# Attention inside a fused kernel: low-rank columns joined to the values, maxima turned in one transpose, masks and products in another order

## The chip, the cores and the metric

One core of one Trainium2 chip. The metric is the device time of one execution in microseconds.

## The reference, cut to what matters

Eight sequences of 512 rows by 512 columns pass through a state-space block `s` and, beside it, a transformer block whose gated output multiplies it. The change lies in the transformer block's attention and in the small low-rank modulation of its gate:

```python
x = _rmsnorm(hidden_states, ln1_w)
attn = _attention(x, Wq, Wk, Wv, Wo)      # 16 heads of 32, causal, softmax
mod = MOD_SCALE * jnp.tanh(attn @ A)      # A is 512 x 16
h = _rmsnorm(residual, ln2_w)
gate_pre = h @ W_in_base.T + mod * (h @ A) @ B
gate = jax.nn.silu(gate_pre)
up = h @ W_up_base.T
mlp_out = gate * up @ W_down.T
return residual + mlp_out
```

`attn` is needed only as `attn @ A`, so the kernel folds Wv, Wo and A into 16 columns a head: the values have 16 heads x 16 = 256 columns.

## The kernel before, in words

The kernel has three stages: the state-space block (to about 821 us), attention (to about 1462 us) and the feed-forward part with the output. FP32 products are made as three FP32R matmuls each: high by high, high by low, low by high (`project3`, lines 72 to 74). "Batch" below is one of the 8 sequences.

In attention each engine walks one list, `steps` (lines 1369 to 1453). It is laid out by hand: `at(third, kind, ...)` puts a step into a third of a head; a head has three thirds, a batch of 16 heads has 48, a word w is four heads. Within a third the order is that of the `at` calls. Each engine takes from the list the steps that concern it, strictly in order; semaphores join them. Per head:

- **weights**: key blocks J against queries, transposed scores into banks 4 and 5. The thirds hold J = 0 (512 columns), J = 1 and 3 (384 + 128), J = 2 (256). Behind each product one bf16 matmul of the identity with a triangle of 0 and -1e30 adds the causal mask to the 128 diagonal columns (lines 1747 to 1753). ScalarE takes the exponential (L1851), then casts all 1280 columns to FP16 (L1856). VectorE subtracts to get the remainder (L1922); POOL does its last 256 columns in the first seven batches (L2016).
- **largest**: six heads ahead, the untransposed scores (L1730) into banks 2 and 3, query block 3 (512 columns), then 2 and 0 (384 + 128), then 1 (256). VectorE masks them and takes the row maximum, one instruction a block (L1915), into `MX`. TensorE may write a bank again when the third two before has been reduced (`maxima`, L1725).
- **largest_in**, **largest_out**, once a word: four transposes turn `MX` (L1738), ScalarE negates them into a 4x512 tile (L1835), and a DMA puts them as row 96 under the queries (L1843), so that the weights' product subtracts the maximum.
- **mixed**: two heads later, the FP16 probabilities (high and remainder) times the bf16 values, 20 matmuls of 50 columns (L1768, L1770). It comes last in the first third of a head. **drawn**, **inverse**, **divided**, **summed**, **gathered** divide by the row sums and add up the heads.

Between them, for the next batch, in banks 0 and 1: **normal** (transposes of the input, thirds -3 to 3), **project** (queries and keys, L1707 to L1709), **values** (thirds 14, 17, 26, 35; 256 columns, through `project3`), and **low_rank** (third 45): 12 matmuls that give `h @ A` turned, as 16x512, which ScalarE copies to `HA` (L1830). Banks 0 and 1 pass from user to user by the list `frees01`. VectorE turns copies into remainders (L1891, L1898, L1905).

**modulation**, once a batch, third 11 of the batch that follows (third 17 for batch 6, in the feed-forward list for batch 7): four transposes of the summed attention `AM` (L1796), tanh to a 16x512 tile (L1879), VectorE multiplies it by 0.1 and `HA` (L1957), ScalarE copies it twice to `MS` (L1884, L1885), VectorE stores the remainder (L1962).

The feed-forward stage has its own list (`ffn_order`, L2056); its TensorE is busy nearly all the time. The last batch's modulation stands there after column 4.

Of the kernel before, what the change touches and what calls it, by code (L numbers as in the profile page):

```python
# [32 lines left out]
def build(nc, x, WinT, convw, convb, WxT, Alog, dtb, outWT, Dp, ln1, ln2, WqT, WkT, Wv, Wo, Aw, Bw, WgT, WuT, WdT,  # L33
          ident, umask, arow, maskt, maskT, out):
    ctx = ExitStack()
    with ctx:
# [1229 lines left out]
        def fast_pool(pool):  # L1266
# [38 lines left out]
        (a_xs, a_tr, a_rh, a_rl, a_pj, a_qh, a_ql, a_vl, a_vh, a_v1, a_vp, a_lr, a_ha, a_lg, a_mx, a_ti, a_ni, a_wt, a_ex, a_ph,  # L1305
         a_rm, a_rp, a_pv, a_ao, a_nu, a_sm, a_tm, a_th, a_mo) = sems(
            "a_xs a_tr a_rh a_rl a_pj a_qh a_ql a_vl a_vh a_v1 a_vp a_lr a_ha a_lg a_mx a_ti a_ni a_wt a_ex a_ph "
# [18 lines left out]
        VW = [sb(at_, f"VW{i}", [128, 4, 256], F32R) for i in range(2)]  # L1326
        AW = [sb(at_, f"AW{i}", [128, 4, R], F32R) for i in range(2)]
# [17 lines left out]
        NM = [sb(at_, f"NM{i}", [4, S], F32R) for i in range(2)]  # L1345
        HA = [sb(at_, f"HA{i}", [R, S]) for i in range(2)]
# [3 lines left out]
        TH = sb(at_, "TH", [R, S])  # L1350
# [18 lines left out]
        for third in range(-72, 3 * HEADS + 24):  # L1369
            g, p = divmod(third, 3)  # L1370
            if 0 <= g < HEADS:
                at(third, "weights", third, ((0,), (1, 3), (2,))[p])
            if 0 <= g + 6 < HEADS:
                at(third, "largest", third + 18, ((3,), (2, 0), (1,))[p])
# [5 lines left out]
            if p == 0 and 0 <= g - 2 < HEADS:  # L1380
                at(third, "mixed", g - 2)
            if p == 1 and g % 2 and 0 <= g - 3 < HEADS:
                at(third, "drawn", (g - 3) // 2)
        for b in range(NB):
# [22 lines left out]
            bank_of["low_rank", b] = 1  # L1407
            at(t + (45 if b else 44), "low_rank", b)
# [47 lines left out]
        for kind, a, how in steps:  # L1456
# [6 lines left out]
            elif kind == "low_rank":  # L1463
                key, free = (kind, a), (a_ha, a + 1)
            elif kind == "largest_in":
                key, free = (kind, a), (a_ni, a + 1)
            elif kind == "modulation":
                key, free = (kind, a), (a_th, 3 * a + 1)
# [10 lines left out]
        maxima = [1, 3, 4]  # L1479
# [70 lines left out]
        def prep_scalar(act, part):  # L1550
# [7 lines left out]
            if part == 5:  # L1558
                for k in range(4):
                    act.wait_ge(a_pp, 2 + k // 2)  # L1560
                    act.activation(VW[0][:, k, :], values_weights(k), ACT.Identity, scale=L1C[:, k:k + 1]).then_inc(a_pa, 1)
            if part == 6:
                for k in range(4):
                    act.activation(AW[0][:, k, :], AF[:, k, :], ACT.Identity, scale=L2C[:, k:k + 1]).then_inc(a_pa, 1)
# [873 lines left out]
```

## Time and profile before

| | us |
|---|---|
| median of 3 runs | 2537.52 |
| lowest, highest | 2536.71, 2538.83 |
| span of the profiled execution | 2534.2 |
| median less that span | 3.3 |
| TensorE busy in the span | 2475.4 |
| VectorE busy | 1370.8 |
| ScalarE busy | 1060.8 |
| POOL busy | 474.7 |

The profiled execution is known by its span, from the first to the last instruction of the program; its own whole time is not listed, so it is set beside the median of the runs. Busy time is the union of an engine's instructions. TensorE's ends are modelled, and its matmuls overlap: the pace is the distance between two starts. PE, PEld, DVE, ACT and POOL are TensorE, its weight loads, VectorE, ScalarE and GpSimd; L1730 is a line of the kernel.

### The profile page before, as it was taken

How to read it: one execution, taken by the hardware profiler on the slowest of the kernel's cores; microseconds unless marked ns; L12 is line 12 of the kernel's file. 1: busy time of each engine (PE TensorE's matmuls, PEld its weight loads, DVE VectorE, ACT ScalarE, POOL GpSimd, SP SyncE). 2: the span in 40 equal slices, each digit the busy share in tenths (PEclk: the TensorE clock that was granted, in tenths of full speed). 3: DMA queues.
4: the chain of work that ended last, by engine and by line, in shares of the span. 5: the costliest groups of instructions: out<-in, count | busy, mean ns of one | idle time of the engine just before them, and what ended most of it. 6: DMA issues, size and time to landing. Idle time of an engine off the chain costs nothing.

```text
span 2534.2 us, 38406 instructions
## 1 busy us (share of the span) xinstructions
PE 2475.4 (98%) x14359; PEld 1996.5 (79%) x14359; DVE 1370.8 (54%) x2860; ACT 1060.8 (42%) x1767; POOL 474.7 (19%) x430
## 2 busy tenths in 40 slices
PE   7999999999999999999999899999999999999998
PEld 5878888878878777777777678888888788888887
DVE  7756757667655688888888842122224323222323
ACT  6444454544544477777777731111112211111111
POOL 4000000000002254444443600000000202222222
PEclk9999999999999999999999999999999999999999
DMA  4010100000003776666666320111113312222212
GB/s 143 18 34 1 34 34 1 34 17 18 17 17 114 222 205 183 199 195 177 192 179 166 106 88 28 44 51 50 50 50 125 125 46 96 100 96 100 96 67 83
DMA packets 106971, 228.12 MB, mean 90 GB/s; under 512 B 14976, under 2 KB 15488, under 8 KB 100624
## 3 DMA queue, kind: packets, MB, share of 16 engines
q1 hardware_dynamic: 105056, 225.31, 27.9%
q8 instruction: 120, 1.97, 0.3%
q14 instruction: 67, 0.55, 0.1%
q10 hardware_dynamic: 1728, 0.29, 0.1%
HBM read 149.77 MB, written 75.50 MB: 89 GB/s over the span
## 4 chain that ended last, share of the span: by engine, by line
PE 89%; DVE 6%; issue 3%; ACT 2%; DMA 0%; POOL 0%; SPq 0%; DVEq 0%; ACTq 0%; POOLq 0%
PE PS L72 14%; PE PS L74 14%; PE PS L73 13%; PE PS L2227 4%; PE PS L2228 4%; PE PS L2229 4%; PE PS L1730 3%; PE PS L1749 3%; PE PS L1707 3%; PE PS L811 2%; PE PS L812 2%; PE PS L813 2%; PE PS L1709 2%; PE PS L1708 2%; PE PS L797 1%
## 5 line engine op out<-in xcount | busy, mean ns | idle before, releaser
L2296 DVE TENSOR_TENSOR SG<-SG,PS 128x512 f32<-128x512 f32 x124 | 85.2, 687 | 642.1 <-PE PS L74 640.1
L74 PE MATMUL PS<-FH,GU 128*128 128x512 f32 x992 | 388.7, 392 | 0.0
L72 PE MATMUL PS<-FH,GU 128*128 128x512 f32 x992 | 387.8, 391 | 0.2 <-DVE DW L2287 0.2
L73 PE MATMUL PS<-FL,GU 128*128 128x512 f32 x992 | 387.9, 391 | 0.0
L1915 DVE CUSTOM_DVE_ANT_0 PS<-PS,MK 128x512 f32<-128x512 f32 (+3 forms) x512 | 243.6, 505 | 86.0 <-PE PS L1730 85.0
L2266 ACT ACTIVATE SG<-PS 128x512 f32<-128x512 f32 x124 | 74.0, 597 | 466.8 <-PE PS L2203 465.2
L2332 POOL TENSOR_SCALAR XN<-XT,MEAN,RSTD 128x512 f32<-128x512 f32 x32 | 69.5, 2171 | 940.0 <-DMA M<-m_scratch 940.0
L1851 ACT ACTIVATE PF<-PS 128x512 f32<-128x512 f32 (+1 forms) x384 | 199.4, 526 | 79.9 <-PE PS L1751 78.4
L2269 ACT CAST GH<-SG 128x512 fp32r<-128x512 f32 x124 | 76.9, 620 | 349.6 <-DVE SG L2296 349.6
L72 PEld LDWEIGHTS PS<-FH,GU 128*128 128x128 f32 x992 | 186.7, 188 | 41.1 <-ACT SG L2266 0.6
L73 PEld LDWEIGHTS PS<-FL,GU 128*128 128x128 f32 x992 | 186.6, 188 | 40.9
L74 PEld LDWEIGHTS PS<-FH,GU 128*128 128x128 f32 x992 | 186.8, 188 | 39.9
L72 PE MATMUL PS<-XH,WH 128*128 128x512 f32 x504 | 208.9, 415 | 0.0
L2227 PE MATMUL PS<-DW,GH 128*128 128x512 f32 x500 | 195.5, 391 | 4.1 <-DVE GL L2298 4.1
L74 PE MATMUL PS<-XH,WL 128*128 128x512 f32 x504 | 197.7, 392 | 0.0
L73 PE MATMUL PS<-XL,WH 128*128 128x512 f32 x504 | 197.0, 391 | 0.0
L2229 PE MATMUL PS<-DW,GL 128*128 128x512 f32 x500 | 195.4, 391 | 0.0
L2228 PE MATMUL PS<-DW,GH 128*128 128x512 f32 x500 | 195.4, 391 | 0.0
L1922 DVE TENSOR_TENSOR PL<-PF,PH 128x1024 f16<-128x1024 f32 (+1 forms) x128 | 178.0, 1391 | 4.7 <-ACT PH L1856 4.7
L1730 PE MATMUL PS<-KS,QS 96*128 96x512 f32 (+3 forms) x512 | 169.9, 373 | 10.8 <-DVE MX L1915 10.6
L1749 PE MATMUL PS<-QS,KS 97*128 97x512 f32 (+3 forms) x512 | 165.4, 353 | 4.4 <-ACT PF L1851 2.7
L1856 ACT CAST PH<-PF 128x1280 f16<-128x1280 f32 x128 | 161.3, 1260 | 4.1
(299 smaller groups left out, 5312.6 us busy)
## 6 DMA issues: line engine op xcount, KB each, us to landing
qk_scratch<-QT SPq DMA_DIRECT2D x128, 256.0 KB, 4.6
QS<-qk_scratch SPq DMA_DIRECT2D x96, 256.0 KB, 4.0
KS<-qk_scratch SPq DMA_DIRECT2D x96, 256.0 KB, 4.1
FH<-rh_scratch SPq DMA_DIRECT2D x16, 1024.0 KB, 5.8
FL<-rl_scratch SPq DMA_DIRECT2D x16, 1024.0 KB, 7.7
XF<-in_x_dram SPq DMA_DIRECT2D x32, 256.0 KB, 4.1
s_scratch<-ZS SPq DMA_DIRECT2D x8, 1024.0 KB, 4.3
rh_scratch<-RH SPq DMA_DIRECT2D x8, 1024.0 KB, 10.2
```

Source lines behind the costliest of these rows:

```text
L72: pe.matmul(o, lh(k), xh(k), start=open_ and k == 0, stop=False, skip_group_check=True)
L73: pe.matmul(o, lh(k), xl(k), start=False, stop=False, skip_group_check=True)
L74: last = pe.matmul(o, ll(k), xh(k), start=False, stop=close and k == nk - 1, skip_group_check=True)
L1730: t = pe.matmul(p[:, at:at + n], QS[0:96, h, 128 * k:n], KS[0:96, h, 0:n], start=True, stop=True, skip_group_check=True)
L1749: pe.matmul(p[:, at:at + n], KS[0:97, h, 128 * J:128 * J + 128], QS[0:97, h, 128 * J:512], start=True, stop=False, skip_group_check=True)
L1851: act.activation(PE_[u][:, o:o + at], PS[4 + a % 2][:, 0:at], ACT.Exp, scale=SC).then_inc(a_ex, 1)
L1856: act.copy(PH[u][:, :], PE_[u][:, :]).then_inc(a_ph, 1)
L1915: dve.tensor_tensor_reduce(out=p[:, at:at + n], in0=p[:, at:at + n], in1=MK[:, 512 - n:512], scale=1.0, scalar=NEG, op0=ALU.add, op1=ALU.m ...
L1922: dve.tensor_tensor(PL[u][:, 0:n], PE_[u][:, 0:n], PH[u][:, 0:n], ALU.subtract).then_inc(a_rm, 1)
L2227: pe.matmul(PS[4 + k][:, :], GH[g][:, c], DW[:, f, 0, :], start=f == 0, stop=False, skip_group_check=True)
L2228: pe.matmul(PS[4 + k][:, :], GH[g][:, c], DW[:, f, 1, :], start=False, stop=False, skip_group_check=True)
L2229: t = pe.matmul(PS[4 + k][:, :], GL[g][:, c], DW[:, f, 0, :], start=False, stop=f == 7, skip_group_check=True)
```

## The change

1. Low rank: `A` becomes 16 more columns of the values' weights `VW` (272 columns), and the step `low_rank` goes. ScalarE copies the 16 columns of each of the four row blocks to `HA`, now 128 x 4 x 16. VectorE's `values_low` waits for it too.
2. Modulation in the same layout: tanh on 128x64 (`bounded`, third 10), times `HA` (`modulated`, third 11), then the four transposes (third 20, bank 0; batch 6 as before third 17 in bank 1), copies and remainder straight from the bank.
3. Maxima: `MX` is ordered so that one transpose turns all 16 columns; the negated tile is 16x128.
4. `mixed` is first in its third, ahead of weights.
5. Query block 0 of the maxima moves from the second third to the last, ahead of that third's weights; it opens the bank, and block 1 joins it behind the weights. `maxima` is 1, 2, 4 in place of 1, 3, 4.
6. Masks: with one key block the mask matmul comes first and opens the bank; with two (J = 1 and 3) one matmul of two 128-column blocks, 256 columns apart, closes it. Three mask matmuls a head in place of four.

```diff
@@ in the layout of the steps @@
         for third in range(-72, 3 * HEADS + 24):
             g, p = divmod(third, 3)
+            if p == 0 and 0 <= g - 2 < HEADS:
+                at(third, "mixed", g - 2)
+            if p == 2 and 0 <= g + 6 < HEADS:
+                at(third, "largest", third + 18, 0)
             if 0 <= g < HEADS:
                 at(third, "weights", third, ((0,), (1, 3), (2,))[p])
             if 0 <= g + 6 < HEADS:
-                at(third, "largest", third + 18, ((3,), (2, 0), (1,))[p])
+                at(third, "largest", third + 18, (3, 2, 1)[p])
...
-            if p == 0 and 0 <= g - 2 < HEADS:
-                at(third, "mixed", g - 2)
...
-            bank_of["low_rank", b] = 1
-            at(t + (45 if b else 44), "low_rank", b)
...
-            m, bank_of["modulation", b] = (107, 0) if b + 2 < NB else (113, 1)
+            m, bank_of["modulation", b] = (116, 0) if b + 2 < NB else (113, 1)
             if b + 1 < NB:
+                at(t + 106, "bounded", b)
+                at(t + 107, "modulated", b)
                 at(t + m, "modulation", b)
-                at(t + m + 1, "modulated", b)
-                at(t + m + 2, "modulation_out", b)
-                at(t + m + 3, "modulation_low", b)
+                at(t + m + 1, "modulation_out", b)
+                at(t + m + 2, "modulation_low", b)
...
-        maxima = [1, 3, 4]
+        maxima = [1, 2, 4]
@@ TensorE @@
-                    project3(pe, p[:, 0:256], lambda k: RH[:, k, c], lambda k: RL[:, k, c],
+                    project3(pe, p[:, 0:272], lambda k: RH[:, k, c], lambda k: RL[:, k, c],
                              lambda k: VW[0][:, k, :], lambda k: VW[1][:, k, :], 4).then_inc(a_vl, 1)
-                elif kind == "low_rank":
-                    p = own01(kind, a)
-                    project3(pe, p[0:R, :], lambda k: AW[0][:, k, :], lambda k: AW[1][:, k, :], rh, rl, 4).then_inc(a_lr, 1)
                 elif kind == "largest":
                     w, j = divmod(a // 3, 4)
-                    h, at, p = 4 * (w % 4) + j, 0, PS[2 + a % 2]
-                    if a >= 2:
+                    h, at, n = 4 * (w % 4) + j, 256 if how == 0 else 0, 128 * how + 128
+                    if a >= 2 and how != 1:
                         pe.wait_ge(a_mx, 4 * ((a - 2) // 3) + maxima[(a - 2) % 3])
...
-                    for k in how:
-                        n = 128 * k + 128
-                        t = pe.matmul(p[:, at:at + n], QS[0:96, h, 128 * k:n], KS[0:96, h, 0:n], start=True, stop=True,
-                                      skip_group_check=True)
-                        at += n
-                    t.then_inc(a_lg, 1)
+                    t = pe.matmul(PS[2 + a % 2][:, at:at + n], QS[0:96, h, 128 * how:n], KS[0:96, h, 0:n], start=how != 1, stop=True,
+                                  skip_group_check=True)
+                    if how:
+                        t.then_inc(a_lg, 1)
                 elif kind == "largest_in":
                     p = own01(kind, a)
                     pe.wait_ge(a_mx, 16 * a + 16)
-                    for k in range(4):
-                        t = pe.transpose(p[0:4, 128 * k:128 * k + 128], MX[a % 2][:, k, :], idn[:, :])
-                    t.then_inc(a_ti, 1)
+                    pe.transpose(p[0:16, 0:128], MX[a % 2][:, :, :].rearrange("p j k -> p (j k)"), idn[:, :]).then_inc(a_ti, 1)
...
+                    blocks = p[:, :].rearrange("p (c q) -> p c q", q=128)[:, 0:len(how) * 3 - 2:3, :]
+                    triangles = MR[:, :].unsqueeze(1).to_broadcast([128, len(how), 128])
+                    if len(how) == 1:
+                        pe.matmul(blocks, idb[:, :], triangles, start=True, stop=False, skip_group_check=True)
                     for J in how:
                         n = 512 - 128 * J
-                        pe.matmul(p[:, at:at + n], KS[0:97, h, 128 * J:128 * J + 128], QS[0:97, h, 128 * J:512],
-                                  start=True, stop=False, skip_group_check=True)
-                        t = pe.matmul(p[:, at:at + 128], idb[:, :], MR[:, :], start=False, stop=True, skip_group_check=True)
+                        t = pe.matmul(p[:, at:at + n], KS[0:97, h, 128 * J:128 * J + 128], QS[0:97, h, 128 * J:512],
+                                      start=len(how) == 2 and at == 0, stop=len(how) == 1, skip_group_check=True)
                         at += n
+                    if len(how) == 2:
+                        t = pe.matmul(blocks, idb[:, :], triangles, start=False, stop=True, skip_group_check=True)
                     t.then_inc(a_wt, 1)
...
                 elif kind == "modulation":
                     p = own01(kind, a)
-                    pe.wait_ge(a_sm, sm(4 * a + 3, 4))
+                    pe.wait_ge(a_mo, 2 * a + 1)
                     for k in range(4):
-                        t = pe.transpose(p[0:R, 128 * k:128 * k + 128], AM[:, k, :], idn[:, :])
+                        t = pe.transpose(p[0:R, 128 * k:128 * k + 128], TH[:, k, :], idn[:, :])
@@ ScalarE @@
                 elif kind == "values":
...
+                    if a >= 2:
+                        act.wait_ge(a_mo, 2 * (a - 2) + 1)
+                    act.copy(HA[a % 2][:, how, :], bank01(kind, a, how)[:, 256:272]).then_inc(a_ha, 1)
...
+                elif kind == "bounded":
+                    act.wait_ge(a_sm, sm(4 * a + 3, 4))
+                    act.wait_ge(a_tm, a)
+                    act.activation(TH[:, :, :], AM[:, :, :], ACT.Tanh).then_inc(a_th, 1)
@@ VectorE @@
                 elif kind == "largest":
...
-                    for k in how:
-                        n = 128 * k + 128
-                        dve.tensor_tensor_reduce(out=p[:, at:at + n], in0=p[:, at:at + n], in1=MK[:, 512 - n:512], scale=1.0,
-                                                 scalar=NEG, op0=ALU.add, op1=ALU.max,
-                                                 accum_out=MX[w % 2][:, k, j:j + 1]).then_inc(a_mx, 1)
-                        at += n
+                    dve.tensor_tensor_reduce(out=p, in0=p, in1=MK[:, 512 - n:512], scale=1.0, scalar=NEG, op0=ALU.add,
+                                             op1=ALU.max, accum_out=MX[w % 2][:, j, how:how + 1]).then_inc(a_mx, 1)
...
                 elif kind == "modulated":
                     dve.wait_ge(a_th, 3 * a + 1)
-                    dve.wait_ge(a_ha, a + 1)
-                    dve.scalar_tensor_tensor(out=TH[:, :], in0=TH[:, :], scalar=0.1, in1=HA[a % 2][:, :],
+                    dve.wait_ge(a_ha, 4 * a + 4)
+                    dve.scalar_tensor_tensor(out=TH[:, :, :], in0=TH[:, :, :], scalar=0.1, in1=HA[a % 2][:, :, :],
                                              op0=ALU.mult, op1=ALU.mult).then_inc(a_mo, 1)
```

## Rows read from the trace of the kernel before

**Rows 1.** The page, part 1: busy time, share of the span, instructions.

```profile
PE 2475.4 (98%) x14359; PEld 1996.5 (79%) x14359; DVE 1370.8 (54%) x2860; ACT 1060.8 (42%) x1767; POOL 474.7 (19%) x430
```

**Rows 2.** Windows: stretch, length, busy time of each engine, granted clock, DMA share, GB/s.

```profile
857.00:860.40 3.40, 3.40 (x13) 2.46 (x14) 2.44 (x10) 1.17 (x2) 0.00 (x0) 0.52 1.00 408
...
1070.48:1106.03 35.55, 34.65 (x338) 25.80 (x336) 30.95 (x88) 27.43 (x47) 14.46 (x16) 1.00 0.68 194
1030.87:1070.48 39.61, 38.91 (x371) 30.89 (x369) 33.05 (x89) 29.86 (x50) 19.92 (x22) 1.00 0.62 184
1388.24:1462.12 73.88, 65.24 (x645) 49.54 (x645) 63.14 (x131) 53.59 (x88) 48.22 (x42) 0.98 0.35 109
```

**Rows 3.** Waits of TensorE from 864 to 1388 us: total, times, longest.

```profile
PE PS L1730 <- DVE MX L1915: 5.4, 9, 0.7
```

**Rows 4.** Timeline of TensorE: start, duration, instruction.

```profile
1000.21 0.48 PE L1707 MATMUL PS<-RH,QW 128*128 128x512 f32 x1
1000.53 0.39 PE L1708 MATMUL PS<-RL,QW 128*128 128x512 f32 x1
...
1000.99 0.34 PE L1749 MATMUL PS<-QS,KS 97*128 97x384 f32 x1
1001.17 0.23 PE L1751 MATMUL PS<-MR,idb 128*128 128x128 bf16 x1
1001.21 0.31 PE L1749 MATMUL PS<-QS,KS 97*128 97x128 f32 x1
1001.36 0.23 PE L1751 MATMUL PS<-MR,idb 128*128 128x128 bf16 x1
1001.40 0.48 PE L1730 MATMUL PS<-KS,QS 96*128 96x384 f32 x2
1001.72 0.44 PE L1707 MATMUL PS<-RH,QW 128*128 128x512 f32 x1
1002.00 0.40 PE L1708 MATMUL PS<-RL,QW 128*128 128x512 f32 x1
...
1003.54 0.39 PE L1749 MATMUL PS<-QS,KS 97*128 97x512 f32 x1
1003.77 0.23 PE L1751 MATMUL PS<-MR,idb 128*128 128x128 bf16 x1
1003.81 0.48 PE L1730 MATMUL PS<-KS,QS 96*128 96x512 f32 x1
...
1004.13 0.20 PE L1768 MATMUL PS<-VB,PH 128*128 128x50 bf16 x1
```

**Rows 5.** Timeline of TensorE: the transposes of the maxima, four in one row.

```profile
1004.65 0.60 PE L1738 MATMUL PS<-idn,MX 128*4 128x128 f32 x4
```

**Rows 6.** Timelines around the low rank: TensorE's first, its successor, VectorE's instruction behind it.

```profile
1008.67 0.39 PE L72 MATMUL PS<-RH,AW 128*16 128x512 f32 x1
...
1011.42 0.60 PE L1697 MATMUL PS<-idn,STGB 128*128 128x128 f32 x4
...
1012.79 0.57 DVE L1915 CUSTOM_DVE_ANT_0 PS<-PS,MK 128x384 f32<-128x384 f32 x1 [2.01 <-PE PS L1730]
```

**Rows 7.** Timeline of TensorE: products of the values, before the first head.

```profile
829.11 0.28 PE L72 MATMUL PS<-VW,RH 128*128 128x256 f32 x1
829.22 0.28 PE L73 MATMUL PS<-VW,RH 128*128 128x256 f32 x1
```

**Rows 8.** Groups from 988 to 1064 us: ScalarE's copy of the values.

```profile
L1821 ACT CAST VB<-PS 128x256 bf16<-128x256 f32 x4 | 1.5, 370 | 1.2 <-PE PS L74 1.2
```

**Rows 9.** Timeline at the last modulation, in the feed-forward stage.

```profile
1474.54 0.68 DVE L2287 TENSOR_TENSOR DW<-STGC,DW 128x512 fp32r<-128x512 f32 x1
...
1476.10 0.60 PE L1796 MATMUL PS<-idn,AM 128*16 128x128 f32 x4
```

**Rows 10.** Timelines of POOL and TensorE: a remainder and the products behind it.

```profile
1090.37 1.71 POOL L2016 TENSOR_TENSOR PL<-PF,PH 128x256 f16<-128x256 f32 x1 [6.08 <-ACT PH L1856]
...
1092.73 0.20 PE L1768 MATMUL PS<-VB,PH 128*128 128x50 bf16 x1
```

More of the change, by code:

```diff
@@ L1325, in build @@
         QW = [sb(at_, f"QW{i}", [128, 4, 512], F32R) for i in range(4)]
-        VW = [sb(at_, f"VW{i}", [128, 4, 256], F32R) for i in range(2)]
-        AW = [sb(at_, f"AW{i}", [128, 4, R], F32R) for i in range(2)]
+        VW = [sb(at_, f"VW{i}", [128, 4, 256 + R], F32R) for i in range(2)]
         STGB = sb(at_, "STGB", [128, 2048])
@@ L1344, in build @@
         MX = [sb(at_, f"MX{i}", [128, 4, 4]) for i in range(2)]
-        NM = [sb(at_, f"NM{i}", [4, S], F32R) for i in range(2)]
-        HA = [sb(at_, f"HA{i}", [R, S]) for i in range(2)]
+        NM = [sb(at_, f"NM{i}", [16, 128], F32R) for i in range(2)]
+        HA = [sb(at_, f"HA{i}", [128, 4, R]) for i in range(2)]
         on = ExitStack()
@@ L1349, in build @@
         on.close()
-        TH = sb(at_, "TH", [R, S])
+        TH = sb(at_, "TH", [128, 4, R])
         RD = sb(at_, "RD", [128, 16])
@@ L1467, in build @@
             elif kind == "modulation":
-                key, free = (kind, a), (a_th, 3 * a + 1)
+                key, free = (kind, a), (a_mo, 2 * a + 2)
             elif kind == "gate" and how == 0:
@@ L1598, in prep_vector @@
                     dve.wait_ge(a_pa, 10 + k // 2 * 2)
-                    low(VW[1][:, k, :], values_weights(k), L1C[:, k:k + 1], VW[0][:, k, :])
+                    low(VW[1][:, k, 0:256], values_weights(k), L1C[:, k:k + 1], VW[0][:, k, 0:256])
             if part in (5, 6):
@@ L1610, in prep_vector @@
                     dve.wait_ge(a_pa, k + 13)
-                    low(AW[1][:, k, :], AF[:, k, :], L2C[:, k:k + 1], AW[0][:, k, :])
+                    low(VW[1][:, k, 256:272], AF[:, k, :], L2C[:, k:k + 1], VW[0][:, k, 256:272])
             if part == 8:
@@ L1825, in attn_scalar @@
                     act.copy(BS[32 * a:32 * a + 16, :], STGA[1][0:R, :]).then_inc(a_pa, 1)
-                elif kind == "low_rank":
-                    act.wait_ge(a_lr, a + 1)
-                    if a >= 2:
-                        act.wait_ge(a_mo, 2 * (a - 2) + 1)
-                    act.copy(HA[a % 2][:, :], bank01(kind, a)[0:R, :]).then_inc(a_ha, 1)
                 elif kind == "largest_in":
@@ L1908, in attn_vector @@
                     w, j = divmod(a // 3, 4)
-                    at, p = 0, PS[2 + a % 2]
+                    n, at = 128 * how + 128, 256 if how == 0 else 0
+                    p = PS[2 + a % 2][:, at:at + n]
                     dve.wait_ge(a_lg, a + 1)
@@ L1933, in attn_vector @@
                     dve.wait_ge(a_sm, sm(a, 2))
-                    dve.wait_ge(a_tm, a // 4)
+                    if a % 4 == 0 and a:
+                        dve.wait_ge(a_th, 3 * (a // 4) - 2)
                     dve.tensor_reduce(dst[:, :, :], NU[:, :, :].rearrange("p (h k) r -> p k r h", k=4), AX.X,
```

38 lines of the change are left out of this document (16 added, 22 removed).

## The prediction

> **What bounds the kernel now.** I first read the shares of the page: TensorE is busy 98% of the span, VectorE 54%, ScalarE 42% [rows 1]. That average mixes stages. The change touches only the attention stage (about 821 to 1462 us), so I cut it with the window view: into one batch of 16 heads, 75.2 us, in two stretches, and the last batch. In the first stretch, 35.55 us, the last four heads of one batch and the first four of the next, TensorE is busy 34.65 and VectorE 30.95. In the second, 39.61 us, the eight heads between, they are busy 38.91 and 33.05 [rows 2]. So TensorE sets the time in both, but in the first VectorE is only 4.6 us behind. Then the waits: over seven batches TensorE waits for VectorE's maxima 5.4 us [rows 3]. Last the timeline of TensorE, because "busy" there hides weight loads: a matmul is listed from its issue, so what counts is the distance from one start to the next.
>
> **Order and masks, per head, on TensorE.** In the first third of a head a 512-column product takes 0.23 (1003.54 to 1003.77), the 128-column mask 0.04, and the 512-column product behind it 0.32 (1003.81 to 1004.13): 0.09 of it is the FP32 weight load that so short a matmul cannot cover. The products with the values are as short, and the projection after them takes 0.32 too (1000.21 to 1000.53) [rows 4]. Afterwards the values come first, the mask follows them and the key product pays one uncovered load for both: 0.09 saved. In the second third 0.99 to 2.00 is 1.01 us: 384 columns 0.18, mask 0.04, 128 columns 0.15, mask 0.04, then 384 and 128 columns 0.32, and the projection's first 0.28 [rows 4]. Afterwards: 0.18, 0.06 for 128 columns, the joined mask of 256 columns, 384 columns 0.18, projection 0.23. No row shows a two-block bf16 matmul; it is at least its neighbour's 0.04 and at most two masks with an uncovered load each, 0.26; I take 0.13, one mask with its load, the nearest row. Sum 0.78, and 0.06 for the 128-column product that goes to the last third: 0.17 saved. In the last third that product and the opening mask change places with nothing else; I count zero. Together 0.26 us per head; the bounds of the joined mask make it 0.13 to 0.35.
>
> What the Trainium skill says bears on this. Its page "TensorE: Matmul & The Clock Gate", section "LDWEIGHTS", gives a load of 128 columns as 128/1.2, about 107 ns, which would leave only some 54 ns uncovered behind a 128-column mask, not the 90 of the rows. By the page alone a head would save an estimated 0.17 and the total would come out near 2506; the trace disagrees, and I go by it.
>
> **Transposes of the maxima.** Four of 128 columns span 0.60 with 0.27 for one, so 0.11 each [rows 5]. Three of four go, four times a batch: 1.3 us. The copy behind them shrinks from 4x512 to 16x128, on ScalarE, off the path.
>
> **Low rank.** It was 12 matmuls of 512 columns, 1008.67 to 1011.42: 2.75 us in each batch [rows 6]. In its place the values' products grow from 256 to 272 columns. 256 take 0.11 [rows 7]; 16 more are 16/256 of that, 7 ns, times 48: 0.34. Were the weight load to cover them it would be nothing; the upper end, 0.02 each, is 1.0. ScalarE gets four more copies of 128x16 a batch. The nearest row, 128x256, has 370 ns [rows 8]; that is 1.5 at most, against a 16x512 copy less, and ScalarE is busy only 27.4 of 35.6 us [rows 2]. VectorE now waits for that copy before it reads the values' bank; the same engine's copy of the values comes after it anyway.
>
> **Modulation.** As many transposes (0.35 us) as before; inside a batch they move from third 11 to third 20, between the maxima's transposes in bank 0 and the projection of third 24, so out of my first stretch into the second. No DMA moves with them, and SP and POOL pass nothing. For the last batch TensorE now waits until tanh and the product with the low-rank part are done. Before, VectorE ended its last weight split at 1475.22 and TensorE came to these transposes at 1476.10 [rows 9]. The new 128x64 product, some 0.2 to 0.4, fits between. If that cover were gone, the four down products behind it would stand, for less than a microsecond.
>
> **Sum.** TensorE's need in a batch falls by 16 x 0.26 = 4.2, plus 1.3, plus 2.75, less 0.34: 7.9 us. That is not what the time falls by, for VectorE's work hardly changes.
> First stretch: 35.55 less 0.90 idle, 8 x 0.26, 0.66, 2.75 and 0.35 leaves TensorE 28.8. VectorE has 30.95 and becomes the bound. During the low-rank matmuls it stood idle 2.01 us [rows 6]; that hole closes. It won't be perfectly fed; with 1.3 us of idle left I get 32.3, 3.3 saved.
> Second stretch: 39.61 less 2.1 and 0.66, plus 0.34 and 0.35, is 37.5 for TensorE with its old waits in it, above VectorE's 33.05. For tighter bank handovers I add 0.5: 38.1, 1.5 saved.
> 4.8 per batch, seven times: 33.6. The lead-in before the first head loses one low-rank block of 2.75, but the first scores must then wait for their maxima to land: 2.0 (0 to 3). In the last batch, 73.88 us with TensorE busy 65.24 and VectorE 63.14 [rows 2], the work falls by about 5 us but waits for ScalarE, VectorE and POOL rule: 2.0 (0 to 5). The stage behind is untouched: 0. Total 37.6. The profiled span is 2534.2; the median of the runs, 2537.5, stands 3.3 above it, and what lies around the span does not change. Forecast 2537.5 - 37.6 = **2500 us**, its own range 2493 to 2508.
>
> **Rivals.**
> *Fully elastic* (0.18). The two score banks let TensorE run ahead far enough to keep VectorE full. For it: VectorE is busy 87% of the first stretch already, and its largest hole there is the low-rank block [rows 2, 6]. First stretch 31.0, second 37.5: 4.5 + 2.1, times 7 is 46, with 2.5 and 3 at the ends: 2486.
> *The values come too early* (0.21). POOL's remainder ends at 1092.08 and the products that need it start at 1092.73 [rows 10]; now they start some 0.6 us earlier in the head (what stood before them, 1003.54 to 1004.13), and earlier still without the low-rank block. The wait goes from covered to real and TensorE cannot run ahead. At 0.1 us a head that takes 1.6 from a batch's 4.8: 3.2 x 7 = 22, 2 at the ends: 2513. Against it: POOL's remainder took 1.71 us there, the longest I found in the batch, and where VectorE is the bound already the same wait is not paid twice.
> *It does nothing* (0.04). If VectorE's idle time stays wherever it is and only moves, the stage keeps its pace and TensorE waits instead: within 5 us of 2537.
> *The clock falls* (0.04), the slower side. A TensorE that waits for VectorE is idle more. Between 857.0 and 860.4, in the lead-in, where it waits for maxima more often, the granted clock was 0.52, so nearly all at the lower level of 1.2 GHz [rows 2]; 3.4 us of such work is 1.7 us lost. Above 22 such stretches the gain of 37.6 is gone. Four a batch in the VectorE-bound heads would be 28, 48 us lost: 2548. Against it: the first stretch has TensorE at 28.8 of 32.3, its waits are short, and the clock there is 1.00 now. The same page of the Trainium skill, in its part on the clock gate, says that idleness lowers the clock and that short idle times between groups can make it swing; this trace shows it only in the lead-in.
>
> **How the numbers follow.** The forecast has 0.53. The range reaches from the elastic case to past the early-values case: 2486 to 2517; the bounds of the joined mask (2 us a batch in the second stretch at most) lie inside. A measurement can tell about 0.2%, 5 us, from no change. Faster by more: 0.53 + 0.18 + 0.21 = 0.92; same 0.04; slower 0.04.
>
> **What would show it.** Right: no 16-column-weight block between heads; about 34 us less between the first and the last batch; VectorE above 93% in the eight heads around a batch's start; products after the values at 0.23; three mask matmuls a head; more waits of TensorE for maxima. Wrong: a joined mask far above 0.13; waits of the values' products for the remainder in most heads; granted clock below 1.00 in the batches; VectorE under 88% in the first stretch.

## The result, and the profile after

The kernel with the change takes 2521.53 us (median of 4 runs, 2520.57 to 2522.03), the kernel before on the same chip 2537.23 (2536.71 to 2538.83). The ratio is 0.9936, with a 95% interval of 0.9922 to 0.995: 16 us gained. I had forecast 2500 and a range up to 2517, so the sign was right and the size was more than twice too large. The profiled execution has a span of 2520.0 against 2534.2.

Busy time on the page, part 1, of the kernel after:

```profile
PE 2435.9 (97%) x14039; PEld 1985.8 (79%) x14039; DVE 1350.7 (54%) x2860; ACT 1056.2 (42%) x1791; POOL 453.2 (18%) x430
```

TensorE lost 39.5 us of busy time against [rows 1] and the span shrank by 14.2. The work that I meant to remove is gone; two thirds of it did not turn into time. Cutting both traces at the first product of a head with its keys (512 columns) gives the places. The feed-forward stage is counted here from its first gate product (1455.2 after), some 8 us later than in [rows 2]:

| stretch, us | before | after | change | forecast |
|---|---|---|---|---|
| input of attention to head 0 | 42.94 | 42.65 | -0.3 | -2.0 |
| seven batches | 523.6 | 504.1 | -19.5 | -33.6 |
| last batch, its first 12 heads | 54.87 | 60.48 | +5.6 | |
| from there to the feed-forward stage | 27.27 | 26.13 | -1.1 | |
| last batch, both lines above | 82.14 | 86.61 | +4.5 | -2.0 |
| feed-forward stage | 1063.8 | 1064.8 | +1.0 | 0 |

The window view of the kernel after, which answers to [rows 2]. First line: 6.8 us across the end of the lead-in and the start of head 0. Second: the four heads on each side of a batch start. Third: the eight between. Fourth: the last batch's first 71.6 us. The two last lines are pieces of it.

```profile
863.70:870.50 6.80, 6.10 (x25) 5.24 (x26) 3.98 (x16) 3.87 (x6) 0.00 (x0) 0.50 1.01 221
1065.71:1098.70 32.99, 29.75 (x312) 23.18 (x308) 30.18 (x89) 27.41 (x47) 11.65 (x15) 1.00 0.67 193
1026.46:1065.71 39.25, 37.92 (x367) 31.42 (x363) 31.02 (x88) 29.52 (x54) 20.19 (x22) 1.00 0.63 180
1368.57:1440.16 71.59, 62.81 (x547) 49.66 (x543) 55.13 (x124) 47.34 (x79) 42.95 (x40) 0.81 0.35 111
1368.90:1389.40 20.50, 18.79 (x133) 14.84 (x132) 16.05 (x43) 12.76 (x21) 16.02 (x15) 0.50 0.76 231
1403.00:1409.80 6.80, 5.72 (x32) 4.46 (x33) 3.50 (x12) 1.13 (x2) 6.45 (x7) 0.50 0.33 113
```

The first stretch went from 35.55 to 32.99, and VectorE is busy 91% of it: near my 32.3. The second went from 39.61 to 39.25 where I had 38.1: TensorE is idle 1.3 us there, and VectorE, at 79%, is no bound. The last batch has a mean granted clock of 0.81 where it was 0.98: 27 us of it at 1.2 GHz, against 3.4 before.

All waits of TensorE over 1 us in the seven batches after:

```profile
PE PS L1705 <- DVE V L1899: 10.8, 21, 0.8
PE PS L1723 <- DVE MX L1908: 6.9, 21, 0.7
PE PS L1764 <- DVE PL L1913: 5.0, 13, 0.4
PE PS L1764 <- issue: 2.6, 6, 0.4
PE PS L1730 <- DVE MX L1908: 2.3, 6, 0.4
PE PS L72 <- DVE QT L1891: 1.3, 7, 0.3
PE PS L1741 <- DMA QS<-NM: 1.1, 1, 1.1
```

Before, the same view had 5.4 us for the maxima [rows 3] and two lines more:

```profile
PE PS L72 <- DVE QT L1898: 2.1, 5, 0.4
PE PS L1707 <- DVE V L1905: 1.9, 7, 0.3
```

So TensorE's listed waits grew from 9.4 to 30 us. Three kinds are new or larger: the projection waits for bank 1, which VectorE's remainder of the values holds (from 1.9 to 10.8); the products with the values wait for VectorE's remainder of the probabilities (L1764, from 0 to 5.0, and 2.6 more put down to issue); and the maxima's products wait in more and smaller pieces.

TensorE, two thirds of a head in which it waits for nothing, from the first product with the values to the projection in the second third (start, duration, instruction; rows left out are marked):

```profile
1044.95 0.20 PE L1764 MATMUL PS<-VB,PH 128*128 128x50 bf16 x1
...
1045.71 0.22 PE L1741 MATMUL PS<-MR,idb 128*128 128x128 bf16 x1
1045.74 0.48 PE L1744 MATMUL PS<-QS,KS 97*128 97x512 f32 x1
1046.06 0.39 PE L1723 MATMUL PS<-KS,QS 96*128 96x512 f32 x1
1046.29 0.39 PE L1705 MATMUL PS<-RH,QW 128*128 128x512 f32 x1
...
1046.98 0.40 PE L1744 MATMUL PS<-QS,KS 97*128 97x384 f32 x2
1047.22 0.28 PE L1748 MATMUL PS<-MR,idb 128*128 128x256 bf16 x1
1047.26 0.42 PE L1723 MATMUL PS<-KS,QS 96*128 96x384 f32 x1
...
1047.76 0.39 PE L1706 MATMUL PS<-RL,QW 128*128 128x512 f32 x1
```

The steps that I priced per head are all there. The key product pays the one uncovered load (1045.74 to 1046.06, 0.32) and the next 512-column product takes 0.23. The second third takes 0.78 (1046.98 to 1047.76), my number. What I did not price stands on VectorE. Its idle time before the 512-column maximum, in batches 1 to 5 together, is the last figure of each of these rows; the first is of the kernel before, the second of the kernel after, the third of first_only, the kernel before with nothing changed but the values first:

```profile
L1915 DVE CUSTOM_DVE_ANT_0 PS<-PS,MK 128x512 f32<-128x512 f32 x80 | 55.6, 695 | 39.6 <-PE PS L1730 39.6
L1908 DVE CUSTOM_DVE_ANT_0 PS<-PS,MK 128x512 f32<-128x512 f32 x80 | 56.0, 700 | 52.4 <-PE PS L1723 52.4
L1915 DVE CUSTOM_DVE_ANT_0 PS<-PS,MK 128x512 f32<-128x512 f32 x80 | 55.9, 699 | 66.6 <-PE PS L1730 66.6
```

The products with the values (1044.95 to 1045.71) now run ahead of the 512-column product that VectorE waits for. VectorE waited there before, too, in 8 heads of 16 and for 7.9 us a batch; with the values first it is 10.5 us. Its next step in the head is the remainder L1913, which the next products with the values need, so that comes later too.

### The profile page after: what moved, and what is told of

The parts are those of the page before. It is cut to its first block, busy times and chain, and to the rows that moved or that the text cites. A ratio compares the mean times of both kernels' runs of the same rounds, so it can differ in the third digit from the quotient of the medians.

```text
span 2520.0 us, 38024 instructions
## 1 busy us (share of the span) xinstructions
PE 2435.9 (97%) x14039; PEld 1985.8 (79%) x14039; DVE 1350.7 (54%) x2860; ACT 1056.2 (42%) x1791; POOL 453.2 (18%) x430
## 4 chain that ended last, share of the span: by engine, by line
PE 86%; DVE 8%; issue 4%; ACT 2%; DMA 1%; SPq 0%; POOL 0%; DVEq 0%; ACTq 0%; POOLq 0%
PE PS L72 14%; PE PS L74 13%; PE PS L73 13%; PE PS L2219 4%; PE PS L2220 4%; PE PS L2221 4%; PE PS L811 2%; PE PS L812 2%; PE PS L813 2%; PE PS L1744 2%; PE PS L1705 2%; PE PS L1723 2%; PE PS L1707 2%; PE PS L1706 2%; PE PS L797 1%
## 5 line engine op out<-in xcount | busy, mean ns | idle before, releaser
L1844 ACT ACTIVATE PF<-PS 128x512 f32<-128x512 f32 (+1 forms) x384 | 201.1, 529 | 102.1 <-PE PS L1744 57.5
L2324 POOL TENSOR_SCALAR XN<-XT,MEAN,RSTD 128x512 f32<-128x512 f32 x32 | 68.7, 2147 | 941.5 <-DMA M<-m_scratch 941.5
L1913 DVE TENSOR_TENSOR PL<-PF,PH 128x1024 f16<-128x1024 f32 (+1 forms) x128 | 167.1, 1305 | 3.9 <-ACT PH L1849 3.9
```

The costliest lines, as they stand in the source:

```text
L1844: act.activation(PE_[u][:, o:o + at], PS[4 + a % 2][:, 0:at], ACT.Exp, scale=SC).then_inc(a_ex, 1)
L1913: dve.tensor_tensor(PL[u][:, 0:n], PE_[u][:, 0:n], PH[u][:, 0:n], ALU.subtract).then_inc(a_rm, 1)
```

## The experiments

"Pace" and "waits" in this table are mine, from TensorE's timeline, the mean of batches 1 to 5. The distance from one start to the next beyond 0.36 us (0.34 for operands under 384 columns, 0.05 for the values with the high probabilities) counts as a wait, the rest as pace. It misses waits shorter than that, so it serves to compare kernels only, and it comes from one execution of each. "Last" is the last batch's first 12 heads. All times are medians, beside the kernel before on the same chip.

| kernel | us | ratio, 95% | pace | waits | last |
|---|---|---|---|---|---|
| before | 2537.2 | 1 | 73.6 | 1.6 | 54.9 |
| after | 2521.5 | 0.9936 [0.9922, 0.995] | 67.6 | 4.3 | 60.5 |
| low_only | 2525.8 | 0.9958 [0.9944, 0.9972] | 71.1 | 1.7 | 61.0 |
| masks_only | 2534.3 | 0.9991 [0.9982, 1.0] | 72.1 | 2.4 | 54.0 |
| first_only | 2558.1 | 1.0083 [1.0069, 1.0097] | 73.6 | 3.6 | 57.5 |
| both_back | 2524.4 | 0.9954 [0.994, 0.9967] | 70.5 | 1.2 | 59.5 |
| mask_back | 2541.0 | 1.0014 [1.0005, 1.0024] | 70.9 | 3.4 | 62.1 |
| mixed_last | 2517.7 | 0.9922 [0.9905, 0.9939] | 68.7 | 3.5 | 58.7 |
| mod_early | 2521.5 | 0.9936 [0.992, 0.9953] | 67.5 | 4.4 | 57.3 |
| mod_mixed | 2511.9 | 0.9898 [0.9881, 0.9914] | 68.3 | 2.5 | 54.9 |

**Parts done alone on the kernel before.** low_only has the low rank in the values' weights and the modulation in its layout (the 1st and 2nd part of the change); its maxima still take four transposes a word.

> The kernel before with only the low rank among the values' columns and the modulation in that layout; order, masks, maxima and their transposes as before. Theory (clock and VectorE as the bound): the hole of 2.0 us in VectorE closes in each of seven batches, about 2 us each, and the last batch has the halved clock already, since the block of head 111 is gone too: 2524 to 2530. Rival (waits of the new order): without the new order the last batch keeps its length, and the time is at or below the kernel after, 2512 to 2521.

It measured 2525.8, 11.5 us faster than before, inside the range of the first theory. Batches 1 to 5 of its trace take 72.8 in the mean for 75.2. masks_only and first_only are parts 6 and 4 alone; this is the edit of first_only:

```diff
+            if p == 0 and 0 <= g - 2 < HEADS:
+                at(third, "mixed", g - 2)
             if 0 <= g < HEADS:
                 at(third, "weights", third, ((0,), (1, 3), (2,))[p])
...
-            if p == 0 and 0 <= g - 2 < HEADS:
-                at(third, "mixed", g - 2)
```

> The kernel before with only the masks of the kernel after: first where there is one key block, joined where there are two. Theory (TensorE sets the pace of most heads, so its work counts nearly in full): the 0.13 us a head that joining saves, and a little where the opening mask no longer stands between two FP32R products: 12 to 18 us, 2519 to 2525. Rival (VectorE takes the bound over and hides it): at most 6 us, 2531 or above.

> The kernel before with only the products with the values first in their head's first third. Theory (the values first hold back the products that VectorE waits for, by some 0.5 us a head, and with them the remainder, the values' low part and bank 1): slower than the kernel before, 2540 to 2550. Rival (the order only saves an uncovered weight load where a mask precedes, and costs nothing): 2534 to 2539.

The masks alone gave 2534.3, 3 us, at the edge of what can be told, where my theory had 12 to 18 and the rival at most 6. Values first alone gave 2558.1: a **loss of 21 us**, 8 beyond what I had expected even of the slower theory; its trace has 16 of them in the seven batches. TensorE's waits in first_only, from 864 to 1404 us:

```profile
PE PS L1707 <- DVE V L1905: 11.5, 21, 1.0
PE PS L1768 <- POOL PL L2016: 4.9, 7, 0.7
PE PS L72 <- DVE QT L1898: 3.4, 6, 0.6
PE PS L1768 <- DVE PL L1922: 2.5, 7, 0.4
PE PS L1730 <- DVE MX L1915: 2.4, 8, 0.3
```

They come to 25 us where they were 9.4, and VectorE's idle time before the 512-column maximum grew by 5.4 us a batch (39.6 to 66.6 in five, above). The pace did not improve (73.6 in both); TensorE's timeline shows why:

```profile
1004.76 0.48 PE L1749 MATMUL PS<-QS,KS 97*128 97x512 f32 x1
1005.08 0.23 PE L1751 MATMUL PS<-MR,idb 128*128 128x128 bf16 x1
1005.13 0.48 PE L1730 MATMUL PS<-KS,QS 96*128 96x512 f32 x1
1005.45 0.40 PE L1707 MATMUL PS<-RH,QW 128*128 128x512 f32 x1
```

Both the key product behind the values and the maxima's product behind the mask take 0.32. With the old masks, values first saves no load, it only moves one from the projection to the key product; the 0.09 us belongs to the pair. The line of POOL, seven times 0.7, is the wait that I had seen coming in [rows 10].

**Parts undone in the kernel after.** mask_back puts the four old masks back, mixed_last the values back to the end of their third, both_back does both.

> The kernel after with the masks as before: four a head, each behind its product. Theory (TensorE is the bound in the middle eight heads of a batch, and the joined mask saves about 0.2 us a head there): 1.5 us a batch and some in the rest, 2530 to 2536. Rival (VectorE swallows it everywhere): 2521 to 2525.

> The kernel after, with the products with the values back at the end of a head's first third. Theory (clock): they cost next to nothing where they stand; the batches lose the 0.09 us a head of uncovered weight load again where TensorE is the bound, 2521 to 2527. Rival (the values come too early): the 9 us that TensorE waited for the remainder go, 2512 to 2518.

> After, with the products with the values last in their third again and the old masks behind each product too. With after (2521.5), values last alone (2517.7) and old masks alone (2541.0) this completes the square of the two parts. Theory 'they pay only together': an opening mask with the values last pays an uncovered load twice, so the masks are worth nothing or little here: 2515 to 2520, so values first and masks together cost what they bring. Rival 'the masks bring the same 19 us whatever the order': 2537. Middle, the 3 us that they bring to the kernel before: 2520 to 2522.

| us | old masks | new masks |
|---|---|---|
| values last | 2524.4 | 2517.7 |
| values first | 2541.0 | 2521.5 |

mask_back came out slower than both of its ranges, mixed_last inside the rival's, both_back above the 2515 to 2520 of its theory and the 2520 to 2522 of its middle case, far below its rival. Beside the other parts of the change, the masks bring 6.7 us with the values last and 19.5 with the values first. Values first costs 16.6 with the old masks and 3.8 with the new ones; the intervals of mixed_last and of after overlap, so the times alone make that last figure a likely loss and not a shown one. The traces point the same way: the seven batches take 504.1, 504.8 and 503.5 us in the three kernels that have them as in after (after, mod_early, fill_two) and 501.7, 494.0 and 500.5 in the three that have them as in mixed_last (with mod_mixed and mm_fill, both below). A gain of the size that I counted is excluded. In the pace column values first does save its load once the new masks are there (68.7 to 67.6, 0.07 us a head for my 0.09) and saves nothing with the old ones (70.5 to 70.9). Parts 4 and 6 together brought some 2.9 of the 16 us (the intervals of both_back and after overlap), the rest of the change about 13. TensorE's waits in mask_back and in both_back, same stretch:

```profile
PE PS L1705 <- DVE V L1894: 8.1, 21, 0.7
PE PS L1759 <- DVE PL L1908: 3.8, 14, 0.4
PE PS L1723 <- DVE MX L1903: 3.3, 7, 0.7
```

```profile
PE PS L1723 <- DVE MX L1903: 11.5, 18, 1.3
...
PE PS L1730 <- DVE MX L1903: 1.0, 6, 0.2
PE PS L1705 <- DVE V L1894: 0.4, 1, 0.4
```

The waits for the remainder of the values (8.1 against 0.4) and for that of the probabilities (3.8 against none) come with the values first; so does VectorE's own wait, 60.5 us before the 512-column maxima of batches 1 to 5 in mask_back against 36.1 in both_back (52.4 in after, 40.8 in mixed_last). With the values last TensorE waits for the maxima instead.

**The split of the maxima** (part 5): split_back puts block 0 beside block 2 again.

```diff
-            if p == 2 and 0 <= g + 6 < HEADS:
-                at(third, "largest", third + 18, 0)
...
-                at(third, "largest", third + 18, (3, 2, 1)[p])
+                at(third, "largest", third + 18, ((3,), (2, 0), (1,))[p])
```

> The kernel after, with query block 0 of the maxima beside block 2 in the second third again. Theory (clock): the split is worth at most the weight load it hides behind, time 2520 to 2525. Rival (waits): the later block 0 is what makes TensorE wait for maxima 11 us in all, 2514 to 2518.

It measured 2522.1 (ratio 0.9941 [0.9925, 0.9958]): no difference to after, as the first theory had it. Undone in the fastest version (mm_split_back, below) the time is 2514.2 for 2511.9; the intervals overlap, so no worth of the split is shown.

**The last batch.** VectorE, then TensorE, of the kernel after, some 32 us behind the start of the last batch (rows of their timelines):

```profile
1400.98 1.75 DVE L1945 TENSOR_TENSOR GL<-SG,GH 128x512 fp32r<-128x512 f32 x1
...
1403.30 0.68 DVE L1954 TENSOR_TENSOR MS<-PS,MS 16x512 fp32r<-16x512 f32 x1
```

```profile
1404.08 0.77 PE L1779 MATMUL PS<-FH,GU 128*128 128x512 f32 x1 [3.35 <-issue]
```

The product for a gate (the first feed-forward work, mixed into the last batch) waits 3.35 us and starts 0.10 after VectorE's modulation remainder L1954. Both use bank 1. Before, the modulation held that bank only until tanh had read it; now the copies and the remainder read it, and the remainder stands behind a 1.75 us instruction in VectorE's queue. The wait is in all seven kernels that have the new modulation at its place of third 17 (3.2 to 3.6 us) and in none of the others. In those seven the 12 heads take 58.0 to 62.1 us, in the others 54.0 to 57.5. mod_early moves that one modulation two thirds ahead:

```diff
-            m, bank_of["modulation", b] = (116, 0) if b + 2 < NB else (113, 1)
+            m, bank_of["modulation", b] = (116, 0) if b + 2 < NB else (111, 1)
```

> The kernel after, with batch 6's modulation two thirds earlier (third 15 of the last batch in place of 17; bank 1 in both). In the kernel after, TensorE stands 3.35 us before the second gate column, which needs bank 1, and the clock is halved from there on for 6.8 us. Theory (bank held longer): the bank is now held until VectorE's remainder, where it was free after the tanh; moved away from the gate the wait goes to under 0.5 us and up to 3.4 us of slow clock with it: 2515 to 2518. Rival (something else, as POOL's weights, ends the wait): 2520 to 2523, the wait where it was.

The wait is gone, as expected, and the 12 heads take 57.3 for 60.5, but the median of the runs is 2521.5, the same as after and outside the 2515 to 2518 that I had expected. The profiled span is 2.5 us shorter (2517.5), but that is the fastest run of mod_early beside the slowest of after. So what moved the wait is shown, in the trace, and a gain in the time is not. With the values last the medians do differ (mixed_last 2517.7, mod_mixed 2511.9) and no run of one reaches those of the other, though their intervals still touch.

**The clock.** fill_two adds to the kernel after 12 products of 512 columns, whose results nothing reads, once in the lead-in and once at the start of the last batch, where the clock fell:

```diff
+        for i, (third, bank) in enumerate([(-4, 1), (333, 1)]):
+            bank_of["kept_busy", i] = bank
+            at(third, "kept_busy", i, max(third // 3, 0) % 16)
...
+                elif kind == "kept_busy":
+                    p = own01(kind, a)
+                    for _ in range(12):
+                        t = pe.matmul(p[:, :], QS[0:96, how, 0:128], KS[0:96, how, :], start=True, stop=True,
+                                      skip_group_check=True)
+                    t.then_inc(a_lr, 1)
```

> The kernel after, with 12 products of 512 columns put back into TensorE (2.75 us each time, into the free bank 1, read by nobody) where the first and the last low-rank block stood: just before head 0 and in head 111. Theory (clock): after the change TensorE is idle so often from head 108 on that its clock is halved from 1368.9 to 1389.4 us and again near 1403, and before head 0; with the fillers it is not, and 5.5 us of added work make the kernel faster, 2508 to 2516. Rival (waits): the last batch got longer by the waits that the new order makes, and the clock only follows them; then the fillers cost 0 to 5 us, 2521 to 2526.

It measured 2521.2 (0.9941 [0.9925, 0.9958]), in the rival's range. Windows of fill_two, the last batch's 12 heads and ten microseconds at the end of the lead-in:

```profile
1368.98:1427.98 59.00, 49.41 (x448) 38.00 (x443) 49.29 (x116) 39.41 (x68) 38.22 (x33) 0.88 0.43 135
861.00:871.00 10.00, 9.76 (x58) 7.94 (x59) 7.78 (x28) 5.43 (x10) 0.68 (x1) 1.00 0.91 254
```

The clock of the lead-in is back at 1.00 and about half of the slow stretch of the last batch is gone as well. Twice 2.8 us of added work cost nothing. Either the low clock had cost about as much as that work, or the work fell into time in which TensorE waited anyway; this run can't tell. Filling wins nothing over the kernel after. last_low_short asks whether the old low-rank block had kept the clock up in the kernel before:

```diff
+                    if a < NB - 1:
                         project3(pe, p[0:R, :], lambda k: AW[0][:, k, :], lambda k: AW[1][:, k, :], rh, rl, 4).then_inc(a_lr, 1)
+                    else:
+                        pe.matmul(p[0:R, :], AW[0][:, 0, :], rh(0), start=True, stop=True, skip_group_check=True).then_inc(a_lr, 1)
```

> The kernel before, with 11 of the 12 matmuls of the last low-rank block left out (the low-rank part of the last sequence is not what the reference has). Theory (clock): without that block TensorE is idle enough before the last batch for the clock to be halved for over 6 us there, where it was halved 3.4 us; the 2.5 us of work that go come back as slow clock: 2534 to 2540. Rival (no link): the clock rows stay as in the kernel before and the time falls by about 2 us, 2533 to 2535.

It measured 2535.35 (0.9994 [0.9984, 1.0004]). Its last batch, 12 heads:

```profile
1385.74:1440.66 54.92, 48.18 (x462) 36.41 (x462) 50.19 (x119) 40.04 (x67) 39.32 (x33) 1.00 0.49 145
```

Without the block the granted clock of these heads is 1.00, and they take 54.9 as before at 0.97. So the missing block by itself does not bring the clock down, the rival's case, and the 3.4 us of half clock in the kernel before cost nothing that shows. What brings it down in the kernel after stays open.

**Putting together what helped.** mod_mixed is the kernel after with the values last and the earlier modulation, that is, the diffs of mixed_last and mod_early.

> mod_early and mixed_last together. If both gains are independent, as both theories would have it, 2511 to 2515. If putting the products with the values first had only moved waits about and mixed_last's 4 us are luck of the clock, no better than mod_early alone, 2515 to 2518.

**2511.9 us** (2504.3 to 2513.5), as expected, 25 us below the kernel before and 9.6 below the kernel after, whose interval it does not touch: it beats both. Its profiled run is the fastest of its four by 7 us, so its trace flatters it. Its waits, and its last batch over the same 71.6 us as above:

```profile
PE PS L1723 <- DVE MX L1908: 10.4, 16, 1.0
PE PS L1730 <- DVE MX L1908: 1.6, 6, 0.3
PE PS L1741 <- issue: 1.1, 2, 0.6
PE PS L1705 <- DVE V L1899: 0.9, 1, 0.9
```

```profile
1357.41:1429.00 71.59, 64.11 (x598) 48.58 (x598) 61.86 (x131) 52.06 (x87) 48.44 (x42) 0.91 0.37 112
```

The waits for the remainders are down from 18.4 to 0.9, and those for the maxima are 12.0. VectorE does 61.9 us of work in the 71.6 in which it had done 55.1. Three attempts to better it failed. mm_fill adds 6 products in each of heads 111 and 112; mm_split_back is part 5 undone; mm_join puts the mask of the first third behind its product again:

```diff
-                    if len(how) == 1:
+                    if how == (2,):
                         pe.matmul(blocks, idb[:, :], triangles, start=True, stop=False, skip_group_check=True)
```

> mod_mixed with twice six products of 512 columns (1.4 us each time, read by nobody) in bank 1, in heads 111 and 112. Theory (clock): mod_mixed has 13.7 us at half clock from 1356 us on, around these heads; the fillers prevent most of it and the time is 2506 to 2511. Rival (VectorE, ScalarE and the landing of the maxima set the pace there, and the clock hardly matters): 2512 to 2515.

> mod_mixed with query block 0 of the maxima beside block 2 again. Theory (the split hides one weight load of 128 columns and spreads VectorE's work more evenly): 1 to 4 us slower than mod_mixed, 2513 to 2516. Rival (the split is without effect): 2511 to 2513.

> The version with values last and earlier modulation (2511.9), but the mask of the first third behind its product as before; the mask of the last third stays ahead, the joined one stays. Theory: with the values last, the mask ahead in the first third only opens a second uncovered load (0.08 us a head between the 512-column maxima product and the values): 2506 to 2510, batches 0.5 to 1 us shorter. Rival: the waits for VectorE take it up and the time stays at 2511 to 2513.

mm_fill: 2511.7 (0.9903 [0.9889, 0.9917]), the clock of its last batch (12 heads) at 0.88 all the same, 0.89 in mod_mixed. mm_split_back: 2514.2 (0.9916 [0.9902, 0.9929]). mm_join: 2514.7 (0.9917 [0.9903, 0.993]), pace 69.2 and waits 2.5 against 68.3 and 2.5, so my theory that the opening mask is a loss once the values are last did not come true.

## Why the prediction was wrong

**Order and masks, per head: sized right, paid back.** 0.09 in the first third and 0.17 in the second stand in the trace as I had them (0.32 and 0.23; 0.78 for 1.01). The joined mask takes 0.04 from start to start and its load falls on the product behind it (0.26 for 384 columns), so my 0.13 for both holds. On the load rule of the Trainium skill ("TensorE: Matmul & The Clock Gate", section "LDWEIGHTS"), from which I had estimated 54 ns uncovered: the trace still shows 0.32 against 0.23 for the product that pays, so the row's 90 ns stands.

**The failed step** is that I priced values first on TensorE alone, as a gain of 0.09 us a head. I never asked who waits for the product that they displace. VectorE does: 10.5 us a batch before its 512-column maxima, where it was 7.9 before and 8.2 with the values put back (mixed_last); done alone, values first made it 13.3. Behind that stand its remainders, of the probabilities and of the values, and TensorE then waits for these: 18.4 us over seven batches, 2.6 a batch, against 0.7 in mixed_last. Order and masks together should have taken 4.2 us from a batch. Against the kernel with neither (both_back) the pace falls by 2.9 and the waits grow by 3.1 (1.2 to 4.3), so the batches stay as they were: 71.7 us in both_back, 72.0 in after. The 3.2 that a batch did gain on the kernel before is no more than the low rank, the transposes and the split gain without order and masks (3.5).

My rival "the values come too early" had this mechanism, and its 3.2 us a batch is what was measured, but that is in part luck: it named POOL's remainder, whose wait appears in first_only alone, while in the kernel after it is VectorE's.

How far does this step go? Undoing it gives back 3.8 of the 21.6 us between forecast and result, undoing it together with the modulation's place 9.6. The other 12, from 2511.9 to my 2500, were not taken apart; the largest wait of TensorE left there is that for VectorE's maxima, 12.0 us listed in the seven batches.

**Stretches.** First stretch: forecast 32.3, measured 32.99; the hole of 2.01 us is gone. But the sum behind it is right only in part: I had written that VectorE's work hardly changes, and over a batch it fell from 64.0 to 61.2 us (in one batch its remainder of the probabilities takes 20.2 us for 21.3, and its 128x64 product of the modulation 0.2 for the 1.1 of the 16x512 one), while its idle time in the first stretch is 2.8 and not 1.3. The two errors cancel in part. Second stretch: forecast 38.1, measured 39.25: "For tighter bank handovers I add 0.5" was the mis-sized term, about 1.7 in its place; bank 1 comes free late. Together the two stretches miss 1.85 us a batch, nearly all of the 14 us that the seven batches miss.

**Low rank and transposes: right.** The block of 2.75 is gone. The 16 columns cost 0.25 us a batch in low_only and both_back and 0.47 in after, waits included, for my 0.34. The transposes of the maxima, from start to start, went from 1.41 a batch to 0.10 in both_back, my 1.3, and to 0.56 in after. low_only, which has only the first of these, should save 2.5 a batch and its trace saves 2.3; both_back, which has the transposes and the split as well, saves 3.5. The difference, 1.1, is no more than the transposes alone should bring, so nothing here speaks for a worth of the split; nor did split_back.

**Lead-in:** forecast 2.0, measured 0.3. TensorE's waits there grew from 4.2 to 7.4 us and swallow the block of 2.75: those for the maxima from 2.0 to 3.8, and head 0 now waits for the landing of its negated maxima. TensorE at the first mask:

```profile
864.40 0.29 PE L1741 MATMUL PS<-MR,idb 128*128 128x128 bf16 x1 [1.15 <-DMA QS<-NM]
```

I had foreseen that last wait, inside my 0 to 3. Then 6.8 us run at 0.50 (863.7 to 870.5, the first window above) where it was 3.4; most of that lies in the first batch, which gained only 0.6 us (73.4 to 72.8). I had put a chance of 0.04 on the clock and said that the trace before shows it only in the lead-in; the 0.98 of [rows 2] for the last batch was 3.4 us of it, too.

**Last batch:** forecast -2.0, measured +4.5. "No DMA moves with them, and SP and POOL pass nothing" was true; that copies and remainder now come straight from the bank was the step that I read and did not price. It keeps bank 1 for ScalarE's copies and VectorE's remainder, and the next user of the bank waits 3.35 us. I had looked at the last batch's modulation [rows 9], not at that of batch 6. The rest of the loss goes together with 27 us at 1.2 GHz. How much of it the clock caused is not settled: fill_two bought half of it back and gained nothing.

**In numbers:** of the 21.6 us between forecast and result, the batches have 14, the last batch 6.5, the lead-in 1.7 and the stage behind 1.0; some 2 us go the other way, since the medians differ by 15.7 and the profiled spans by 14.2, and the kernel before itself came out 0.3 lower.

## What to carry to other kernels

When work changes places on a busy engine, price it also on the engine that waits for what is displaced: here an order that should have saved TensorE 0.09 us a head made VectorE wait 0.34 us a head longer when done alone (0.14 beside the other parts), and that came back as TensorE's wait two steps later. Two edits that act on the same uncovered load have to be tried as a pair, since each alone misleads: alone the masks gain 3 us and values first loses 21, while beside values first and the other parts the masks gain 19.5. When a step is rewritten to read its operands straight from a bank, list the next user of that bank at each place where the step stands, the odd one at the end too.

## What I had not expected of the hardware

In these traces TensorE's listed busy time does not tell when the granted clock falls. These are the 8 us just before it fell to 1.2 GHz in the last batch of the kernel after, and 8 us of last_low_short, behind which it stayed at 1.00:

```profile
1360.90:1368.90 8.00, 6.14 (x80) 4.38 (x77) 7.06 (x22) 6.79 (x12) 2.24 (x4) 1.00 0.70 216
1395.00:1403.00 8.00, 6.04 (x51) 4.39 (x48) 8.00 (x18) 5.74 (x9) 7.79 (x6) 1.00 1.02 238
```

TensorE was busy 6.14 us in the one and 6.04 in the other; in both_back the clock fell at 1006.0 behind 8 us with 7.21 of them busy. Once down, in the kernel after, it stayed at 1.2 GHz for 20.5 us (1368.90 to 1389.40), in which TensorE was listed as busy for 18.8. The Trainium skill page "TensorE: Matmul & The Clock Gate", in its part on the clock gate, says that idleness lowers the clock. The fall in the kernel after does follow a stretch with waits, each under a microsecond, but these rows can't tell which idleness counts.

Small transfers land at very different times: the negated maxima, 16x128 elements, landed 2.0 to 7.6 us after issue (median 3.4) in four words of mixed_last in a row. Here the view of that tile:

```profile
L1836 ACTq DMA_DIRECT2D QS<-NM x4: 510/510/526, 1164.4 to 1220.4; - x4
...
DMA to landing us min/median/max: 2.0/3.4/7.6
```

Where TensorE runs further ahead it meets the late one. The view calls these waits of a word's first mask issue, but in mixed_last all six of them (6.2 us together, up to 2.0) end 0.1 us after such a landing; the longest, at 1098.51, behind one that took 8.1 us. mod_mixed, with the same code in these batches, has two of them (1.1 us together). That is 5.1 of the 7.8 us that its seven batches took less in its trace than those of mixed_last, and a reason not to read a few microseconds between two traces as the worth of an edit.
